# A Mamba-style mixer and feed-forward layer on one core: a DMA rate of 300 in the order table, and split weights of u stored one sequence earlier

## The reference

```
proj = x @ W_in.T ; u, gate = halves of proj          # 2048 channels each
u    = silu(causal_conv4(u) + conv_b)
dt, B, C = rmsnorm of the parts of u @ Wx.T           # 64, 16, 16 columns
delta = softplus(dt @ Wdt.T + dt_bias)                # 2048 channels
state = exp(delta * A) * state + (delta * u) * B      # 2048 x 16 states, over 512 steps
y    = (sum_n state * C + u * D_param) * silu(gate)
x    = layernorm(x + y @ W_out.T)
x    = layernorm(x + x @ W.T + b + one of four low-rank products, chosen per row)
```

## Time and profile before

| what | value |
|---|---|
| median of three runs | 2259.97 us (2258.07 to 2263.01) |
| span of the profiled execution, first to last instruction | 2257.2 us |
| PE matmul busy | 2063.3 us, 91% |
| DVE busy | 1986.4 us, 88% |
| POOL busy | 1824.8 us, 81% |
| ACT busy | 1486.3 us, 66% |
| moved by DMA | 354.84 MB, 157 GB/s over the span |

### The profile page before, as it was taken

How to read it: one execution, slowest core, us unless ns; L and a number is a source line. 1 busy time by engine, 2 the same in 40 slices (tenths; PEclk the granted TensorE clock), 3 DMA queues, 4 the chain that set the end, 5 groups by cost and what they waited for, 6 DMA issues and landing times. The chain is left out here.

```text
span 2257.2 us, 30761 instructions
## 1 busy us (share of the span) xinstructions
PE 2063.3 (91%) x10528; PEld 1562.5 (69%) x10528; DVE 1986.4 (88%) x2398; ACT 1486.3 (66%) x2198; POOL 1824.8 (81%) x786
## 2 busy tenths in 40 slices
PE   8989789889999799799998997989999998897998
PEld 6867577778565478687875555867875556785677
DVE  4447779999999999899999999999999999999943
ACT  4478658787666677666886657676786667756531
POOL 4279899998898889768799997979788998698840
PEclk9989899999999999999999998999999999998999
DMA  4466566665333447655463432475463337443340
GB/s 157 138 223 235 204 221 219 203 205 179 92 118 86 126 132 239 209 193 182 158 199 95 111 96 96 147 264 171 143 203 101 110 96 233 148 144 132 101 143 38
DMA packets 168764, 354.84 MB, mean 157 GB/s; under 512 B 18656, under 2 KB 45408, under 8 KB 168608
## 3 DMA queue, kind: packets, MB, share of 16 engines
q1 hardware_dynamic: 168608, 352.87, 48.6%
HBM read 283.96 MB, written 68.85 MB: 156 GB/s over the span
## 5 line engine op out<-in xcount | busy, mean ns | idle before, releaser
L1563 POOL TENSOR_TENSOR drive<-delta_u,b_bcast 128x2048 f32<-128x2048 f32 (+1 forms) x257 | 1172.5, 4564 | 129.1 <-PE state_t L933 120.6
L1115 DVE TENSOR_TENSOR_SCAN drive<-decay,drive 128x512 f32<-128x512 f32 x1024 | 1190.5, 1203 | 62.0 <-POOL drive L1563 37.9
L1355 ACT ACTIVATE decay<-delta,a_sb 128x512 f32<-128x512 f32 x1024 | 694.7, 688 | 377.9 <-DVE drive L1115 374.6
L933 PEld LDWEIGHTS state_t<-identity,drive 128*128 128x128 f32 x4096 | 492.0, 146 | 311.1 <-DVE drive L1115 141.8
L933 PE MATMUL state_t<-identity,drive 128*128 128x128 f32 x4096 | 591.1, 284 | 119.8 <-DVE drive L1115 95.1
L1123 DVE SCALAR_TENSOR_TENSOR y_acc<-state_t,c_rows,y_acc 128x512 f32<-128x512 f32 x727 | 515.3, 734 | 54.3 <-PE state_t L933 51.7
L964 PE MATMUL bank<-cols_high,w_split 128*128 128x512 f32 (+1 forms) x1240 | 524.4, 423 | 26.6 <-POOL w_split L1588 11.8
L966 PE MATMUL bank<-cols_high,w_split 128*128 128x512 f32 (+1 forms) x1240 | 491.8, 397 | 0.0
L965 PE MATMUL bank<-cols_low,w_split 128*128 128x512 f32 (+1 forms) x1240 | 489.6, 395 | 0.0
L987 PE MATMUL bank<-channels,w_raw 128*128 128x512 f32 x896 | 420.2, 596 | 2.3 <-DVE rows L1177 2.0
L1568 POOL TENSOR_TENSOR y_acc<-y_acc,scaled 128x512 f32<-128x512 f32 x233 | 300.1, 1288 | 102.2 <-ACT scaled L1375 101.9
(11 more groups left out here) (204 smaller groups left out, 1451.8 us busy)
## 6 DMA issues: line engine op xcount, KB each, us to landing
w_split<-w_split SPq DMA_DIRECT2D x272, 512.0 KB, 4.0
b_bcast<-b_rows SPq DMA_DIRECT2D x256, 256.0 KB, 3.4
w_raw<-in_w_out SPq DMA_DIRECT2D x112, 256.0 KB, 3.0
w_raw<-in_w_in SPq DMA_DIRECT2D x96, 256.0 KB, 4.1
gates<-scratch SPq DMA_DIRECT2D x64, 256.0 KB, 3.7
scratch<-gates SPq DMA_DIRECT2D x64, 256.0 KB, 4.7
rows<-in_x_rows SPq DMA_DIRECT2D x4, 2048.0 KB, 8.2
out<-rows SPq DMA_DIRECT2D x16, 512.0 KB, 4.8
```

The costliest lines, as they stand in the source:

```text
L933: last = engine.transpose(bank[0:tile.shape[1], i * P:(i + 1) * P], tile, identity[:, :])
L1115: engine.tensor_tensor_scan(state, decay[(GT * s + t) % DECAYS][:, :], state, 0.0, ALU.mult, ALU.add).then_inc(signal["scan"])
L1355: engine.activation(decay[i % DECAYS][:, :], delta[:, g % 2, t, :], ACT.Exp, scale=a_sb[:, j, n:n + 1]).then_inc(signal["decay"])
L1563: engine.tensor_tensor(drive[key % DRIVES][:, tiles, :], du[:, tiles, :], row, ALU.mult).then_inc(signal[stage])
```

## The change

The DMA rate in the order table becomes the constant 300.0 in place of 220.0. The condition that gave u's tiles `keep` 2 is gone, so `keep` is 2 only for tiles from `TILES` on (which have one use and are never stored). Two needs of the table are made strict: a `turn` needs all four scans of its unit instead of the last in number, and a piece whose rival was already taken can't become ready later.

```diff
-IN_HEAD = range(DT)
...
+    RATE = 300.0
...
+                        dropped.add(lost)
...
-                        dma = max(dma, at[e]) + piece["kb"] / 220.0
+                        dma = max(dma, at[e]) + piece["kb"] / self.RATE
...
-                    if left[follower] == 0:
+                    if left[follower] == 0 and follower not in dropped:
...
-        w, keep, pool = (what, n), 2 if what[0] in IN_HEAD or what[0] >= TILES else 1, pool_of(what[0])
+        w, keep, pool = (what, n), 2 if what[0] >= TILES else 1, pool_of(what[0])
...
-            put("PE", i + 4 - TURN_FIRST, 0.45, "turn", (s, tt), [("scan", (s, GT - 1)), *([] if i else [("ssm_norm", 0)])] + (
+            put("PE", i + 4 - TURN_FIRST, 0.45, "turn", (s, tt), [*[("scan", (s, t)) for t in range(GT)], *([] if i else [("ssm_norm", 0)])] + (
...
-                    e.wait_ge(*done("scan", (s, GT - 1)))
+                    for t in reversed(range(GT)):
+                        e.wait_ge(*done("scan", (s, t)))
```

More of the change, by code:

```diff
@@ L162, in arrange @@
         at = {e: 0.0 for e in ENGINES}
-        now, dma, ends, finished, wanted, table = 0.0, 0.0, [], 0, len(self.pieces), None
+        now, dma, ends, finished, wanted, table, dropped = 0.0, 0.0, [], 0, len(self.pieces), None, set()
         for name, piece in self.pieces.items():
```

## The result

The changed kernel takes 2223.78 us (median; 2221.84 to 2226.45) against 2259.73 us for the kernel before in the same rounds: a ratio of 0.9837, with 0.9823 to 0.9851 as its 95% interval. That is 36 us faster.

The account below looks back on a forecast made before the run. DVE was taken as the bound in the middle, with PE full in the head. Terms -2.5 - 6.5 + 3 - 4 = -10 us took the span from 2257.2 to 2247.2, a median of 2250 us; range 2228 to 2274.

Parts of the forecast that it names:

- the rate of 300: Order table, mainly 142 to 285 us: a third of POOL's 12.5 us wait for high parts gained, -4 us.
- 0 for the rest of the run: Where DVE has little idle time, the new rate was taken to give 0, with 8 us either side.
- The head, +3 us: Head, 20 to 88 us: 32 added stores of 512 KB were to cost +3 us, range 0 to +12.
- The rival of a head bound by DMA: Head: DMA paths hold under about 290 GB/s, the stores cost 22 us, total 2269; chance 0.16.
- the old rate would have held the head back: Head: at 220 a tile's 1.5 MB takes the table 7.0 us, over its 5.5 us of PE.
- POOL's relief, -6.5 us: 285 to 527 us: 41 us of splits gone from POOL lets ten sums replace DVE adds, -6.5 us.
- The changeover, -2.5 us: Scan at 297.05 us: two splits in front of its drive go, so the drive starts 2.5 us earlier.
- The strict needs: Order table: the three extra scan waits of a turn are already met and cost nothing.
- the relief is used whole: Rival, 285 to 527 us: relief worth -20 and table -12.5 us, total 2228; chance 0.08.
- PE holds: Rival, 285 to 527 us: PE sets the pace, relief worth only 2.5 us, reordering nothing, total 2260; chance 0.20.
- The table promises too much: Rival: weight transfers land later than the table expects, 19 us on DVE's path, total 2269; chance 0.08.
- signs of error: Wrong if the first scan comes over 10 us later, sums do not rise, or time moves after 640 us.

Follow-up runs that it names:

- rate_only: The changed kernel with u's tiles again kept for two uses (no store in the head, split twice), rate still 300: 2233.01 us, ratio 0.9874.
- The two pairs of the second group: Changed kernel, each pair planned alike in the head, then at 220 or 300 GB/s: unit 24 at 361.5 against 335.9 us, and 380.0 against 353.4.
- tiny_u: The changed kernel in the same order, with u's stores and loads moving only 16 of 1024 columns: 2223.24 us, ratio 0.9832.
- keep_only: The changed kernel with the table's rate back at 220, u's stores still in the head: 2277.56 us, ratio 1.0073.
- pool_again: The changed kernel with a POOL pass over each of sequence 1's 32 loaded halves of u weights, known to the table: 2226.07 us, ratio 0.9845.
- thin_pool: rate_only with POOL's 32 low parts of sequence 1's u weights cut to 16 columns, unknown to the table: 2229.5 us, ratio 0.9856.
- right column: Results of the changed kernel, with u's stores in the head, planned at various rates; at 400 GB/s it took 2236.4 us, ratio 0.989.

## Why the forecast fell short, step by step

**The step that failed is the rate of 300: forecast -4 us, measured -27** (rate_only). I bounded what it could give by one row, the 12.5 us that POOL waited for high parts. That wait did go (0.5 us after), but it was one symptom. The rate decides where in every queue the loads, splits, products and all that hangs on them are written. By its profiled execution the 27 us are 14 on the way to unit 24, 4 in the head and 9 in the tail, and for the last two I had nothing at all. For the stretch, the right bound was all of DVE's idle time from 142 to 363 us, whoever released it: 44.9 us in front of scans and adds, of which rate_only has 35.4 left and the changed kernel 25.6, and 13.6 us more in front of the first scan, of which rate_only has 7.6 left and the changed kernel 7.4. The earlier trace rows held 28.4 us of it in its first line, and I priced the line below. The two pairs of the second group show 26 us made by that stretch's rate alone when the store is in the head.

What the table's path has to do with it can be read from the plan that the programs compute. In the kernel before, the path is busy for the whole of 140 to 363 us of the table's clock, and a transfer waits for it 9.3 us on average from 205 to 285; on the chip the DMA moved 212 to 252 GB/s there. In rate_only it is busy for 74 to 88% and a transfer waits 1.2 to 1.5 us, and the last scan of unit 24 begins at 329.9 us of the table's clock in place of 356.2. At 260 the path is still 90 to 100% busy, but a transfer waits only 2.2 to 3.3 us, and the gain is there. What stays argued is the chain from a late place to the single waits on the chip.

**0 for the rest of the run** missed the tail. With 220 planned there it takes 121.0 to 122.1 us in all four kernels, with 260 to 400 it takes 109.8 to 114.2. The windows of the tail, before and after, show less of PE's work left when the scans end:

```profile
2135.70:2257.20 121.50, 110.75 (x510) 88.88 (x508) 51.37 (x107) 29.40 (x50) 36.67 (x25) 0.97 0.31 94
```

```profile
2111.50:2224.70 113.20, 104.21 (x493) 84.68 (x491) 50.69 (x107) 27.81 (x48) 34.76 (x23) 0.99 0.29 89
```

Between unit 24 and the last scan the lead is 24.9, 33.6 and at last 24.3 us. So there the 0 came true, but a swing of 9 us on the way back to it, and the 15 us between orders at other rates, say that it was in part luck.

**The head, +3 us, is 0.** The rate of flow was forecast as 301 GB/s and is 304, PE stays full, the first scan starts 2.9 us earlier than before and within 1 us of rate_only, which has no stores there, and tiny_u shows no cost of the bytes. The rival of a head bound by DMA is false: its 230 and 255 GB/s were what the written order asked for, and no ceiling. The Trainium skill's rule in "DMA: Bandwidth & Descriptors", section Latency and other measured facts, that access to HBM is slower at high load, fits raw loads that went from 2.7 us at 111 GB/s to 4.3 at 304. It does not fit the 5.3 us at 215 GB/s, nor the pair that I gave as agreeing: 512 KB landed in 3.7 us at 230 GB/s and in 4.7 at 215, the longer time at the lower rate. As PE stayed full, the slot's round stayed under its 10.9 us. The sentence that the old rate would have held the head back was right and deserved a rival of its own: keep_only is that case, slower by 17 us.

**POOL's relief, -6.5 us, is at most 2 to 4.** The sums did rise, from 26 to 34, of which two came with the rate (28 in rate_only). Groups by line after, 285 to 527 us, answering to the earlier trace rows:

```profile
L1126 DVE SCALAR_TENSOR_TENSOR y_acc<-state_t,c_rows,y_acc 128x512 f32<-128x512 f32 x84 | 59.8, 736 | 3.7 <-PE state_t L935 3.5
...
L1571 POOL TENSOR_TENSOR y_acc<-y_acc,scaled 128x512 f32<-128x512 f32 x34 | 43.8, 1289 | 20.4 <-ACT scaled L1378 17.9 <-PE state_t L935 2.5
```

But with 84 adds beside them, 118 turned states in place of 104, the sums' share went only from 25% to 29%, and POOL now waits 20.4 us in front of them. Given back to POOL as work (pool_again) the relief costs 2.3 us, taken from the splits (thin_pool) it gives 3 to 4, and neither is beyond the intervals.

**The changeover, -2.5 us, is too small.** The first convolution of sequence 1's u starts at 299.51 us before, 289.81 in rate_only and 273.97 after. Timelines of rate_only, SP, POOL and DVE:

```profile
261.69 4.03 SPq L829 DMA_DIRECT2D w_raw<-in_x_cols  x4
...
270.31 1.56 SPq L844 DMA_DIRECT2D w_raw<-in_w_in  x2
```

```profile
278.35 5.01 POOL L1591 TENSOR_TENSOR w_split<-w_raw,w_split 128x512 fp32r<-128x512 f32 x4
```

```profile
287.95 1.22 DVE L1118 TENSOR_TENSOR_SCAN drive<-decay,drive 128x512 f32<-128x512 f32 x1 [4.91 <-POOL drive L1566]
289.81 2.31 DVE L1133 SCALAR_TENSOR_TENSOR channels<-bank,conv_w_sb,channels 128x511 f32<-128x511 f32 x3 [0.63 <-ACT channels L1407]
```

and of the changed kernel, SP, POOL and DVE:

```profile
250.37 1.96 SPq L866 DMA_DIRECT2D w_split<-w_split  x2
...
259.16 2.69 SPq L829 DMA_DIRECT2D w_raw<-in_x_cols  x3
```

```profile
266.45 5.02 POOL L1605 TENSOR_TENSOR cols_low<-w_raw,cols_high 128x512 fp32r<-128x512 f32 x4
...
275.18 13.61 POOL L1566 TENSOR_TENSOR drive<-delta_u,b_bcast 128x2048 f32<-128x2048 f32 x3
```

```profile
273.97 4.54 DVE L1133 SCALAR_TENSOR_TENSOR channels<-bank,conv_w_sb,channels 128x511 f32<-128x511 f32 x6 [3.93 <-ACT channels L1407]
280.40 5.67 DVE L1118 TENSOR_TENSOR_SCAN drive<-decay,drive 128x512 f32<-128x512 f32 x5
```

In rate_only the weights come through the same four raw buffers as x's columns, so they are issued from 270.31 us on, behind x, split by 283.4, and DVE waits 4.91 us for a drive that stood behind four splits (no splits of these weights remain in the changed kernel). After, the loads go straight to slots at 250.37 us, ahead of x's last columns, POOL goes from x's low parts over two products for `delta_u` and a sum to three drives in a row, and DVE scans without a wait. I saw two splits in front of one drive; the shared raw buffers I did not see. This cause is argued from the traces and not shown: no run took the buffers apart from the splits, and the 16 us by which the first convolution is earlier do not all reach the end (8 us by the runs at 300).

**The strict needs** were said to cost nothing. Planned at 220 with the old `keep`, the changed program comes out with the order of the kernel before on every engine, so the order owes them nothing; the three extra waits of a turn were not timed by themselves.

**The sum.** Rate -27 for -4, all else together -9 for -6. That the second pair lies close is in part luck: the relief was forecast too large, the changeover too small and the head at 3 us too much. The rival "the relief is used whole" named 2228 us, near the result, for a reason that pool_again refutes. "PE holds" had the small relief about right, and fell by putting the new order at nothing (rate_only). "The table promises too much" does not show at 300; at 400 the time is 12 us longer (right column), which fits it, but which promises were too early is open. Of my own signs of error one came true: time moved after 640 us, in the tail.

## What to carry to other kernels

Where a program writes the order by a table of costs, a constant in it is a change to every queue: bound it by all the waits of the bounding engine in the stretches where that resource is full in the table, and by the tail, not by one wait downstream, and run the constant alone. Here it was safe near what the chip moved (300 to 350, and 260 while no store was in the head), 27 to 54 us dearer at 220, and it decided whether another edit helped or hurt: the same moved store cost 17 us at 220 and gave 8 at 300. Compare waits in windows that hold the same instructions on both sides: a scan that had waited 13.6 us lay inside the window before and outside it after. A low rate in a trace may be what the order asks for, and no limit of the hardware.

## What the runs showed of the hardware

One core's 16 DMA engines carried 304 GB/s for 68 us and 323 for 40 us, mixed 256 KB loads and 512 KB stores from one queue, beside a full PE, and single slices of 1.7 us reached 422 GB/s; I had taken 301 for nine tenths of what they can. Per full share that is 20.61/(0.825 x 68) = 367 GB/s, above the 334 that I had from 285 to 527 us.
